# Second self attention: the maxima products of a step are issued after the value products

## The chip, the cores and the metric

One core of a Trainium2 chip runs the whole program. The metric is the device time of one execution in microseconds (us); lower is better. TensorE is called PE in the profile, its weight loads PEld, VectorE DVE, ScalarE ACT, GpSimd POOL and SyncE SP.

## The reference, cut to what matters

The model has four layers on x of shape (2, 1024, 256), each a cross attention and a feed-forward part with experts. The change lies in the first half of layer 1's feed-forward block, a self attention over 1024 tokens with 16 heads of 16 columns in each of 2 batches:

```python
h = _layernorm(x, ln1_g, ln1_b)
qkv = h @ w_qkv + b_qkv                      # (2, 1024, 768)
q, k, v = jnp.split(qkv, 3, axis=-1)         # 16 heads of 16 columns each
scores = jnp.einsum('bqhd,bkhd->bhqk', q, k) / np.sqrt(DK)
attn = jax.nn.softmax(scores, axis=-1)
o = jnp.einsum('bhqk,bkhd->bqhd', attn, v).reshape(B, S, D)
x = x + o @ w_o + b_o
```

## The kernel before, in words

The stages follow one another, and this attention is the stage `quad_attention` (L1499), called "heads1". It takes the 32 pairs of batch and head in 8 groups of four heads. A group has 16 steps (two halves of 512 queries by 8 blocks of 128 keys), so there are 128 steps, t = 0 to 127.

In a step TensorE makes four **scores** (L1627), each 128 keys by 512 queries for one head. ScalarE takes the exponential of each (L1672) into `probs`. There are three score buffers, so the fourth score of a step waits for the exponential of the first. A step later TensorE multiplies the four probabilities with the **values** (L1636, eight instructions in the trace, four column strips side by side) and accumulates over 8 steps into one buffer, `sums_ps`. At the end of 8 steps ScalarE copies that buffer to `sums` (L1664). That copy stands in ScalarE's order behind the second exponential of step t when t is 9, 17, 25 and so on, and the values issued in that same step (the first of the next eight) wait for it (L1634).

The softmax needs the largest score of each query beforehand. It comes from **peaks**, rough scores in bf16 (L1605): a peak is two products of 128 queries by 512 keys, and VectorE reduces it to two maxima per query (L1688). Each group needs 32 peaks. They are made ahead of their group: 40 before the first step, and two in each of the steps 0 to 107. When a group's peaks are reduced, VectorE makes their negated maxima (L1692), and TensorE **turns** them (TURN, L1610), VectorE splits them into two rows (L1699, L1701), and SP puts them by DMA into rows of `q` (L1580). TURN of group g stands at step 16g - 4. When a group's sums are complete TensorE turns them as well (FOLD, eight transposes, L1614) and VectorE divides them by the row sums (L1711, L1715). FOLD of group g stands at step 16(g + 1) + 2, so 18, 34, up to 114, and the last at the end.

Peaks, TURN and FOLD share one pair of buffers, `shared_ps`, and take them in turn. The function `share` (L1593) issues such an item on TensorE. It first waits until VectorE has read the item before the last:

```python
two = shared_ps[:, used % 2, :, :]
if used >= 2:
    pe.wait_ge(shared_read, used - 1)
```

The lists `work_at[t]` (L1526 to L1532) give the items of each step, the peaks first. TensorE's order is written out at L1644 to L1656. In a step with two peaks and a TURN or a FOLD, the peaks are items 0 and 1 and the other one is item 2. VectorE's and ScalarE's own orders, and SP's, are not touched.

Of the kernel before, what the change touches and what calls it, by code (L numbers as in the profile page):

```python
# [1498 lines left out]
def quad_attention(nc, core, name, q_dram, k_dram, values, q_narrow, k_narrow, out):  # L1499
# [17 lines left out]
    def place(g):  # L1517
        b, c, x = g // 4, g // 2 % 2, g % 2
        return b, c, x

    def heads_of(g):
        b, c, x = place(g)
        return [b * H16 + GH * c + 2 * r + x for r in range(QUAD)]
# [15 lines left out]
    with Stage(nc, name) as st:  # L1539
# [23 lines left out]
        @block.sync  # L1563
        def _(sp):
            def load(g):
                u = g % 2
                n = heads_of(g)
                if g >= 2:
                    sp.wait_ge(score_done, QUAD * PER * (g - 1))
                for i, (q_part, k_part) in enumerate(((0, 0), (0, 1), (1, 0), (1, 1))):  # L1570
                    for dst, src, part in ((q, q_dram, q_part), (k, k_dram, k_part)):
                        sp.dma_start(dst[i * HD16:(i + 1) * HD16, u, :, :].bitcast(F32),
                                     src[part, n[0]:n[-1] + 1:2, :, :].rearrange("h w s -> w h s")
                                     ).then_inc(loaded[u], 16)

            def load_max(g):
                u = g % 2
                sp.wait_ge(max_ready, g + 1)
                for r in range(2):
                    sp.dma_start(q[HL + r:HL + r + 1, u, :, :].rearrange("o h s -> o (h s)").bitcast(F32),  # L1580
                                 max_rows[:, r, :].bitcast(F32)).then_inc(max_loaded[u], 16)

            load(0)
            load(1)
            load_max(0)
            for g in range(1, GROUPS):
                if g >= 2:
                    load(g)
                load_max(g)

        @block.tensor
        def _(pe):
            def share(item):  # L1593
                used = number[item]
# [3 lines that stand above are left out]
                if item[0] == PEAK:  # L1598
                    _, g, s, x, pair = item
                    b, c, odd = place(g)  # L1600
                    for i in range(2):
                        r = 2 * pair + i
                        rows = slice(32 * r, 32 * (r + 1))
                        at = b * S + s * P
                        done = pe.matmul(two[:, i, :], q_narrow[rows, c, at:at + P],  # L1605
                                         k_narrow[rows, odd, c, b * S + x * 512:b * S + (x + 1) * 512],
                                         start=True, stop=True, tile_position=(32 * r, 0))
                elif item[0] == TURN:
                    pe.wait_ge(minus_ready, item[1] + 1)
                    done = pe.transpose(two[0:QUAD * BT, 0, 0:P], minus_max[:], core.ident[:])  # L1610
                else:
                    pe.wait_ge(sums_copied, HALVES * (item[1] + 1))
                    for s in range(BT):
                        done = pe.transpose(two[:, s // 4, s % 4 * P:(s % 4 + 1) * P],  # L1614
                                            sums[:, s // 4, s % 4 * P:(s % 4 + 1) * P], core.ident[:])
                done.then_inc(shared_done, 1)

            def score(t, r):
                g, half, c = t // PER, t % PER // BT, t % BT
                u = g % 2  # L1620
                if t % PER == 0 and r == 0:
                    pe.wait_ge(loaded[u], 16 * LOADS * (g // 2 + 1))
                    pe.wait_ge(max_loaded[u], 32 * (g // 2 + 1))
                i = QUAD * t + r
                if i >= RING:
                    pe.wait_ge(exp_done, i - RING + 1)
                pe.matmul(score_ps[:, i % RING, :], k[:, u, r, c * P:(c + 1) * P],  # L1627
                          q[:, u, r, half * 512:(half + 1) * 512], start=True, stop=True).then_inc(score_done, 1)

            def value(t):  # L1630
                g, c = t // PER, t % BT
                pe.wait_ge(exp_done, QUAD * (t + 1))
                if c == 0 and t:
                    pe.wait_ge(sums_copied, t // BT)  # L1634
                for r, n in enumerate(heads_of(g)):
                    done = pe.matmul(sums_ps[r * SIDE:(r + 1) * SIDE, :], values[:, n, c, :],  # L1636
                                     probs[:, t % SLOTS_OF_PROBS, r, :], start=(c == 0), stop=(c == BT - 1),
                                     tile_position=(0, r * SIDE))
                done.then_inc(value_done, 1)

            pe.wait_ge(ones_done, 1)
            for item in work_at[-1]:
                share(item)
            for t in range(STEPS):  # L1644
                items = work_at[t]
                for r in range(QUAD):
                    score(t, r)
                for item in items[0:2]:
                    share(item)
                if t:  # L1650
                    value(t - 1)
                for item in items[2:]:
                    share(item)
            value(STEPS - 1)
            for item in work_at[STEPS]:
                share(item)  # L1656
# [22 lines left out]
        def _(dve):  # L1679
            def take(item):  # L1680
                used = number[item]
                two = shared_ps[:, used % 2, :, :]
                dve.wait_ge(shared_done, used + 1)
                if item[0] == PEAK:
                    _, g, s, x, pair = item
                    if g >= 2 and (s, x, pair) == (0, 0, 0):
                        dve.wait_ge(minus_ready, g - 1)
# [1441 lines left out]
```

## Time and profile before

| | us |
|---|---|
| median of 3 runs | 2937.05 |
| lowest and highest | 2929.41 and 2939.92 |
| the profiled execution | 2941.6 |
| its span from the first to the last instruction | 2939.9 |
| mean granted clock of TensorE in it | 0.864 of full speed |

The profile is of one execution. Its first part gives each engine's busy time, the second cuts the span in 40 slices; further views give the waits, the instructions in order of time and the busy time of chosen stretches. Times of rows are microseconds from the start of the span. The attention of the change takes the span from 1131 (first peak) to 1591; its 128 steps begin at 1181.5.

### The profile page before, as it was taken

The page shows a single profiled execution, that of the slowest core. Times are in us where ns is not written, and L with a number is a line of the kernel's source. Part 1 is how long each engine was busy: PE and PEld are TensorE (multiplying, and loading weights), DVE is VectorE, ACT ScalarE, POOL GpSimd, SP SyncE. Part 2 cuts the span into 40 slices and gives each one's busy share as a digit, 9 for nine tenths or more (in the row PEclk, how much of TensorE's full clock was granted, in tenths as well). Part 3 has the DMA queues.
Part 4 walks back from the last instruction along what each step waited for, and adds up shares of the span by engine and source line. Part 5 has one row for each costly group of instructions (what it writes and reads, how often), then busy time and mean ns, then how long its engine had stood idle before and what let it go on. Part 6 is the DMA issues. An engine that isn't in the chain of part 4 may idle for free. (4 is left out here: it accounts for less than half of the span.)

```text
span 2939.9 us, 36703 instructions
## 1 busy us (share of the span) xinstructions
PE 2249.7 (77%) x12230; PEld 1326.8 (45%) x12231; DVE 1380.5 (47%) x2584; ACT 1085.4 (37%) x2179; POOL 543.6 (18%) x517
## 2 busy tenths in 40 slices
PE   4989999874485965999998289994938999481597
PEld 2423233223383432233334189992327999231354
DVE  4666666616415358578771500003641000458565
ACT  2413333321131630466675144442613444151211
POOL 0204443440141041000000022220002222104011
PEclk8979999987697885599999599997968999685799
DMA  1000000001351035042420466642046664200001
GB/s 59 1 1 9 12 9 12 12 22 58 116 174 33 1 113 72 4 56 31 58 30 6 145 224 198 197 147 76 1 144 209 199 201 156 72 1 30 9 12 36
DMA packets 145705, 216.37 MB, mean 74 GB/s; under 512 B 39840, under 2 KB 101980, under 8 KB 145580
## 3 DMA queue, kind: packets, MB, share of 16 engines
q1 hardware_dynamic: 135884, 188.27, 23.5%
q0 software_dynamic: 9696, 26.49, 2.4%
q8 instruction: 72, 1.18, 0.2%
q14 instruction: 53, 0.43, 0.1%
HBM read 182.00 MB, written 30.15 MB: 72 GB/s over the span
## 5 line engine op out<-in xcount | busy, mean ns | idle before, releaser
L2840 PE MATMUL experts_up_ps<-experts_rowT,experts_w 128*128 128x128 f32 x2864 | 342.4, 278 | 0.0
L1688 DVE TENSOR_REDUCE heads_part_max<-heads_shared_ps 128x2 f32<-128x1024 f32 x256 | 299.9, 1219 | 90.0 <-PE heads_shared_ps L1605 90.0
L1672 ACT ACTIVATE heads_probs<-heads_score_ps 128x512 f32<-128x512 f32 x512 | 266.4, 602 | 190.7 <-PE heads_score_ps L1627 190.7
L2840 PEld LDWEIGHTS experts_up_ps<-experts_rowT,experts_w 128*128 128x128 f32 x2864 | 334.4, 195 | 0.2
L2990 DVE TENSOR_TENSOR experts_y<-experts_down_ps,experts_b_now 128x256 f32<-128x256 f32 x78 | 33.1, 425 | 557.3 <-PE experts_down_ps L2850 557.3
L2900 ACT ACTIVATE experts_hT<-experts_up_ps,experts_b_now 128x128 f32<-128x128 f32 x624 | 223.2, 368 | 48.3 <-PE experts_up_ps L2840 11.4
L1423 DVE TENSOR_REDUCE heads_part_max<-heads_shared_ps 128x1 f32<-128x367 f32 x384 | 181.1, 532 | 125.8 <-PE heads_shared_ps L1313 125.2
L1627 PE MATMUL heads_score_ps<-heads_q,heads_k 66*128 66x512 f32 x512 | 197.5, 473 | 29.7 <-ACT heads_probs L1672 25.5
L1404 ACT ACTIVATE heads_probs<-heads_score_ps 128x1024 f32<-128x1024 f32 x128 | 131.0, 1024 | 217.8 <-PE heads_score_ps L1340 215.3
L2850 PE MATMUL experts_down_ps<-moe_w,experts_hT 128*128 x808 | 184.5, 379 | 0.0
L2789 POOL DMA_INDIRECT y_dram<-experts_y,experts_index x101 | 99.5, 985 | 456.8 <-DVE experts_y L2990 411.3
L1627 PEld LDWEIGHTS heads_score_ps<-heads_q,heads_k 66*128 66x128 f32 x512 | 92.0, 200 | 198.5 <-ACT heads_probs L1672 163.6
L1352 PE MATMUL heads_sums_ps<-heads_probs,self_values 128*64 128x512 f32 (+1 forms) x576 | 159.1, 630 | 0.3 <-ACT heads_probs L1401 0.2
L2850 PEld LDWEIGHTS experts_down_ps<-moe_w,experts_hT 128*128 128x128 f32 x808 | 148.9, 190 | 17.8
L1340 PE MATMUL heads_score_ps<-self_qT,self_kT 64*128 64x512 f32 (+1 forms) x576 | 155.0, 617 | 0.0
L1636 PE MATMUL heads_sums_ps<-heads_probs,self_values 128*32 128x512 f32 x1024 | 146.8, 647 | 4.1 <-ACT heads_sums L1664 4.1
L2850 PE MATMUL experts_down_ps<-l1f_w,experts_hT 128*128 x624 | 141.0, 379 | 0.0
L873 POOL IOTA gate_offset<- 128x128 f32 x3 | 1.1, 356 | 742.4 <-POOLq L55 742.4
L1279 POOL TENSOR_TENSOR core_xT<-core_xT,heads_probs 128x1024 f32<-128x1024 f32 x48 | 122.6, 2554 | 82.5 <-ACT heads_probs L1404 80.5
L2850 PEld LDWEIGHTS experts_down_ps<-l1f_w,experts_hT 128*128 128x128 f32 x624 | 115.7, 190 | 14.1
L2783 POOL DMA_INDIRECT experts_row<-rows_dram,experts_index x101 | 98.8, 978 | 81.6 <-DVE experts_index L2981 46.2
L2881 ACT ACTIVATE experts_rowT<-experts_rowT_ps 128x256 f32<-128x256 f32 x62 | 23.8, 384 | 242.6 <-PE experts_rowT_ps L2830 242.4
(561 smaller groups left out, 3375.4 us busy)
## 6 DMA issues: line engine op xcount, KB each, us to landing
experts_w<-in_L_ffn_W SPq DMA_DIRECT2D x39, 1024.0 KB, 5.3
experts_w<-in_L_ffn_w SPq DMA_DIRECT2D x39, 1024.0 KB, 5.2
experts_w<-in_L_ffn_W SPq DMA_DIRECT2D x23, 512.0 KB, 4.1
core_xT<-y_dram SPq DMA_DIRECT2D x20, 512.0 KB, 4.8
experts_b_now<-in_L_ffn_b SPq DMA_DIRECT2D x78, 128.0 KB, 3.3
heads_q<-l_queries SPq DMA_DIRECT2D x32, 256.0 KB, 10.1
heads_k<-l_keys SPq DMA_DIRECT2D x32, 256.0 KB, 11.9
l1f_w<-in_L_ffn_W SPq DMA_DIRECT2D x8, 1024.0 KB, 11.8
```

Source lines behind the costliest of these rows:

```text
L1279: pool.tensor_tensor(total, first, probs[:, t % SLOTS_OF_PROBS, :, :], ALU.add).then_inc(pool_added, 1)
L1340: done = pe.matmul(score_ps[0:rows, t % 2, r, :], kT[of, c, b, chunk * P:chunk * P + rows], qT[of, c, queries(t)[1]], start=False, stop=Tr ...
L1352: done = pe.matmul(sums_ps[HW * r:HW * (r + 1), :], values[0:rows, b * spec.heads + 2 * c + r, chunk, :], probs[0:rows, t % SLOTS_OF_PROBS ...
L1404: act.activation(probs[:, t % SLOTS_OF_PROBS, :, :], score_ps[:, t % 2, :, :], ACT.Exp, scale=SC).then_inc(exp_done, 1)
L1423: dve.tensor_reduce(part_max[:, g % 2, r, s, x:x + 1], bank[:, 0:PIECE], AX.X, ALU.max).then_inc(shared_read, 1)
L1627: pe.matmul(score_ps[:, i % RING, :], k[:, u, r, c * P:(c + 1) * P], q[:, u, r, half * 512:(half + 1) * 512], start=True, stop=True).then_ ...
L1636: done = pe.matmul(sums_ps[r * SIDE:(r + 1) * SIDE, :], values[:, n, c, :], probs[:, t % SLOTS_OF_PROBS, r, :], start=(c == 0), stop=(c == ...
L1672: act.activation(probs[:, t % SLOTS_OF_PROBS, r, :], score_ps[:, i % RING, :], ACT.Exp, scale=SC).then_inc(exp_done, 1)
L1688: dve.tensor_reduce(part_max[:, g % 2, 2 * pair:2 * pair + 2, s, x], two, AX.X, ALU.max).then_inc(shared_read, 1)
L2840: done = pe.matmul(up_ps[:, f % 4, 0:SLOT], w1_sb[:, u, c, f * P:(f + 1) * P], rowT[:, u % 2, c, :], start=(c == 0), stop=(c == DC - 1))
L2850: done = pe.matmul(down_ps[:, u % 2, 0:D], hT[:, u % 2, f, :], second.sb[:, bass.ds(e, 1), f, :].rearrange("p o d -> p (o d)"), start=(f = ...
L2900: act.activation(hT[:, u % 2, f, :], up_ps[:, f % 4, 0:SLOT], func, bias=bias).then_inc(act_done, 1)
```

## The change

In each step the two items that stood between the scores and the values are issued behind the values, in front of the next step's scores, together with a third item where there is one. Number and form of all instructions stay the same.

```diff
@@ -1645,11 +1645,9 @@
                 items = work_at[t]
                 for r in range(QUAD):
                     score(t, r)
-                for item in items[0:2]:
-                    share(item)
                 if t:
                     value(t - 1)
-                for item in items[2:]:
+                for item in items:
                     share(item)
             value(STEPS - 1)
             for item in work_at[STEPS]:
```

## Rows read from the trace of the kernel before

**Rows 1.** The page: the span, and TensorE's granted clock in 40 slices

```profile
span 2939.9 us, 36703 instructions
...
PEclk8979999987697885599999599997968999685799
```

**Rows 2.** The waits from 1181 to 1590: in total, times, longest

```profile
ACT heads_probs L1672 <- PE heads_score_ps L1627: 190.7, 128, 58.0
...
PEld heads_shared_ps L1610 <- DVE heads_part_max L1688: 8.3, 7, 1.7
PEld heads_shared_ps L1614 <- DVE heads_part_max L1688: 7.4, 6, 1.2
```

**Rows 3.** In order of time: a plain step at full clock (start, length, engine, instruction)

```profile
1317.35 0.96 PE L1627 MATMUL heads_score_ps<-heads_q,heads_k 66*128 66x512 f32 x3
1318.53 0.49 PE L1627 MATMUL heads_score_ps<-heads_q,heads_k 66*128 66x512 f32 x1 [0.22 <-ACT heads_probs L1672]
1318.96 0.40 PE L1605 MATMUL heads_shared_ps<-self_k_narrow,self_q_narrow 32*128 32x512 bf16 x4
1319.28 1.06 PE L1636 MATMUL heads_sums_ps<-heads_probs,self_values 128*32 128x512 f32 x8
...
1319.39 2.36 DVE L1688 TENSOR_REDUCE heads_part_max<-heads_shared_ps 128x2 f32<-128x1024 f32 x2 [0.58 <-PE heads_shared_ps L1605]
1320.28 0.96 PE L1627 MATMUL heads_score_ps<-heads_q,heads_k 66*128 66x512 f32 x3
```

**Rows 4.** In order of time: a late step without peaks, full clock

```profile
1536.44 0.49 PE L1627 MATMUL heads_score_ps<-heads_q,heads_k 66*128 66x512 f32 x1 [0.22 <-ACT heads_probs L1672]
1536.87 0.16 PEld L1636 LDWEIGHTS heads_sums_ps<-heads_probs,self_values 128*32 128x32 f32 x8 [0.24 <-issue]
```

**Rows 5.** In order of time: step 34 with a FOLD, full clock

```profile
1305.99 0.39 PE L1605 MATMUL heads_shared_ps<-self_k_narrow,self_q_narrow 32*128 32x512 bf16 x4
...
1307.70 1.09 PE L1614 MATMUL heads_shared_ps<-core_ident,heads_sums 128*128 128x128 f32 x8 [0.32 <-DVE heads_part_max L1688]
1308.55 0.95 PE L1627 MATMUL heads_score_ps<-heads_q,heads_k 66*128 66x512 f32 x3
```

**Rows 6.** In order of time: values that wait for the copy, with and without peaks

```profile
1253.52 0.39 PE L1605 MATMUL heads_shared_ps<-self_k_narrow,self_q_narrow 32*128 32x512 bf16 x4
...
1254.15 1.06 PE L1636 MATMUL heads_sums_ps<-heads_probs,self_values 128*32 128x512 f32 x8 [0.24 <-ACT heads_sums L1664]
...
1546.87 0.49 PE L1627 MATMUL heads_score_ps<-heads_q,heads_k 66*128 66x512 f32 x1 [0.23 <-ACT heads_probs L1672]
...
1547.94 1.06 PE L1636 MATMUL heads_sums_ps<-heads_probs,self_values 128*32 128x512 f32 x8 [0.57 <-ACT heads_sums L1664]
```

**Rows 7.** In order of time: step 12 with a TURN, half clock

```profile
1237.60 0.61 PE L1605 MATMUL heads_shared_ps<-self_k_narrow,self_q_narrow 32*128 32x512 bf16 x4
...
1238.15 1.94 PE L1636 MATMUL heads_sums_ps<-heads_probs,self_values 128*32 128x512 f32 x8
...
1240.02 0.40 PE L1610 MATMUL heads_shared_ps<-core_ident,heads_minus_max 128*32 128x128 f32 x1
```

**Rows 8.** Stretches: length, busy PE, PEld, DVE, ACT, POOL, then granted clock, DMA

```profile
1181.00:1240.20 59.20, 58.65 (x202) 18.75 (x202) 30.44 (x27) 27.50 (x53) 0.00 (x0) 0.50 0.00 1
1240.40:1533.00 292.60, 265.04 (x1577) 93.92 (x1575) 233.58 (x220) 202.36 (x393) 0.00 (x0) 1.00 0.37 45
...
244.80:247.00 2.20, 0.03 (x1) 0.00 (x1) 2.20 (x3) 0.80 (x1) 1.94 (x2) 1.00 0.00 0
247.00:250.40 3.40, 3.40 (x9) 1.21 (x11) 1.51 (x5) 0.00 (x0) 1.70 (x1) 0.50 0.04 1
...
461.60:463.60 2.00, 0.01 (x1) 0.01 (x1) 2.00 (x3) 0.59 (x1) 1.74 (x2) 1.00 0.04 12
463.60:467.00 3.40, 3.40 (x18) 1.15 (x18) 2.15 (x7) 0.79 (x1) 1.71 (x1) 1.00 0.04 1
...
978.40:980.00 1.60, 0.00 (x1) 0.03 (x1) 1.39 (x3) 1.39 (x2) 0.00 (x0) 1.00 0.01 5
981.00:984.20 3.20, 3.20 (x17) 0.55 (x16) 1.28 (x1) 1.11 (x2) 0.00 (x0) 0.50 0.00 0
```

**Rows 9.** In order of time: transposes after a stall, layer 1's cross attention

```profile
980.00 1.11 PE L546 MATMUL x_banks<-core_ident,x_minus_max 128*128 128x128 f32 x8 [1.60 <-DVE x_heads_out L774]
```

## The prediction, made before the change was run

> **What bounds the kernel now.** I began with the page: the span of 2939.9 us and the row of TensorE's clock [rows 1]. The stage of the change lies in slices 16 to 22 of the 40, and its first slices stand at 5 tenths of the clock. The stretches say where exactly: from 1181 to 1240.2 the granted clock is 0.50 (1.2 GHz), from 1240.4 to 1533 it is 1.00 (2.4 GHz) [rows 8]. The waits come next. ScalarE waits 190.7 us for scores, once in each of the 128 steps (58.0 of it is one wait ahead of the first) [rows 2]. So ScalarE is not the bound; TensorE's own order is.
>
> Then one plain step in order of time [rows 3]. Scores begin at 1317.35, the fourth at 1318.53 (1.18 later, it waits for the first exponential), peaks at 1318.96 (0.43), values at 1319.28 (0.32), the next scores at 1320.28 (1.00). A step is 2.93 us, and its four parts stand one behind the other on TensorE. VectorE reduces the two peaks in 2.36 us and then idles 0.58 us for the next ones. So it has slack too, though not much.
>
> **The change, part by part.** All prices come from the profiled execution, 2941.6 us as a run, 4.6 above the median of 2937.05. I add the sum to the median.
>
> *Plain steps: nothing.* The order scores, peaks, values becomes scores, values, peaks. Nothing in the step waits for the values sooner (their probabilities are a step old), and nobody waits for the maxima within the step. The three changes from one form of product to another stay three. Fourth score to values without peaks takes 0.43 [rows 4], as fourth score to peaks does [rows 3]. Values to something other than scores shows at half clock: values to TURN is 1.87 [rows 7]. Values to peaks at full clock, and peaks to scores, are not shown in the plain step. The nearest rows are 1.00 (values to scores) and 0.32 (peaks to values) [rows 3], and I take those, so the step stays at 2.93. I allow 0.05 us a step either way, which over the 95 full-clock steps with peaks (13 to 107) is 5 us down or up. VectorE sees the same spacing, so its two waits on `shared_read` stay met.
>
> *Steps with a FOLD: +1.00 each.* The third item must wait until VectorE has reduced the first peak of the same step. Now the values lie between them. In step 34 peaks start at 1305.99, FOLD at 1307.70, so 1.71 later, and TensorE still idles 0.32 after the values [rows 5]. Behind the change the peaks come after the values and FOLD directly behind the peaks. The 1.71 remains, because it is TensorE's peaks plus one reduction, but the values' 1.00 us no longer lies inside it. It now stands ahead. There are six such FOLDs (steps 18 to 98), the six waits of the row for L1614 [rows 2]: 6 x 1.00 = 6.0 us.
>
> *Steps with a TURN: +1.00 each at full clock, +1.35 at half clock.* It is the same wait: seven in the row [rows 2], of which those in steps 12, 28, up to 92 stand behind peaks; the seventh, in step 108, does not. Five run at full clock: 5.0 us. Step 12 is at half clock: peaks to values 0.55, values to TURN 1.87, no wait [rows 7]. After the change TURN can come some 1.9 us behind the peaks (0.65 until the reduction starts, by estimate 0.22 more than at full clock, then half of the 2.36), in place of 0.55 from the peaks to the values: 1.35. TURN's DMA on SP, which brings the maxima into `q`, comes about 1 us later but has four steps to spare. What queues behind the waiting item on TensorE is the next step's scores, and ScalarE behind those.
>
> *Steps with the copy (9, 17, up to 105): +0.32 each.* The values wait for ScalarE's copy. Now the peaks pass ahead of them and fill part of that wait: peaks at 1253.52, values at 1254.15, which is 0.63 and not 0.32. Without peaks the values come 1.07 behind the fourth score and not 0.43 [rows 6]. So the whole wait of 0.64 will be bare where 0.31 was. Thirteen steps at 0.32 make 4.2 us. Steps 113 and 121 have no peaks and stay.
>
> *Other ends.* In step 1 the peaks wait less for VectorE (some -0.3). TURN at 108 and FOLD at 114 only swap with the values: 0.
>
> The sum is 6.0 + 5.0 + 1.35 + 4.2 - 0.3 = 16.3 us, so 2953.4 us, 0.55% more. A measurement of this kernel can tell about 0.5% (14.7 us, so 2922.4 and 2951.7) from no change.
>
> *The clock.* A FOLD step will contain a bare stall. The peaks end some 0.33 behind their start and FOLD comes at 1.71, so 1.38 us without products, then 0.85 us of transposes [rows 5]. In the first attention TensorE did nothing from 244.8 to 247.0 and the clock was 0.50 in the 3.4 us after; another stall, 461.6 to 463.6, was followed by a clock of 1.00 [rows 8]. In layer 1's cross attention 1.60 us of idle time followed by transposes ended in a clock of 0.50 as well [rows 8, 9]. So 1.38 idle and 0.85 of transposes lie near the edge, between a case that fell and one that did not, if transposes keep the clock up as little as idle time does.
>
> The Trainium skill says just that of transposes, in "TensorE: Matmul & The Clock Gate", Part 4: a transpose through TensorE "doesn't count as PE-busy the same way". By that rule FOLD's stall is 2.2 us to the clock, and some FOLDs drop it; if it did not hold, only 1.38 us would count and the sum would stay 2953. The row at 980.00 [rows 9] agrees with it, since the clock fell after 1.60 us of idle plus transposes.
>
> What a fall costs is bounded in two places. In the first attention it lasted 3.4 us, so at most 1.7 us lost. In this attention the loop stayed at half clock from 1181.5 to 1240.0, through steps 0 to 12 [rows 7, 8]: 58.5 us, where 13 plain steps at full clock would be 38.1. That is 20.4 us, 1.57 a step. I take two falls among the six FOLDs, of three steps each, 2 x 3 x 1.57 = 9.4 us: between the two ends, since either row may be the nearer one. The forecast is 16.3 + 9.4, some 25 us over the median, 2962 us. The ends of this term are 0 and about 60 (three falls of 20.4).
>
> **The rivals.**
>
> *Waits only, 2953 us.* The clock does not care for FOLD's 1.38 us of idle. For it: the stall at 461.6 that was followed by full clock. Against it: the falls after 2.2 us and after 1.60 us with transposes [rows 8, 9]. With the 5 us of the unseen changes of form it spans 2948 to 2958. Chance 0.28.
>
> *Long half clock, 2975 to 3013 us.* A fall lasts like the first thirteen steps, 20 us each, one to three of them. For it: in those steps the loop stayed at 0.50 with TensorE busy for 58.65 of 59.20 us [rows 8]. Against: the fall at 247, which was over after 3.4 us, and that the FOLDs are only 16 steps apart, so that three such falls would cover nearly the whole loop. Chance 0.20.
>
> *The clock rises earlier, 2933 to 2942 us, not slower than before.* The steps at half clock at the start are worth up to 20.4 us. If the new neighbours (values and peaks together, then the dense first scores) let the clock rise in the first steps, that pays for the 16.3. It decides from a rise 10 steps (16.3 / 1.57) earlier than now. For it: nothing in the rows says what made the clock rise at 1240.3, and the runs of before spread over 10.5 us. Against: the products per step are the same. Chance 0.10.
>
> **How the numbers follow.** The forecast case (waits, and some short falls, 2955 to 2975) has 0.42. The predicted time is its 2962. The range is 2944 to 2995: below it lies most of the early rise, above it the longer half of the long half clock. Slower by over 0.5%: nearly all of the forecast case, a little over half of waits only, all of long half clock, together 0.70. Faster by over 0.5% needs an early rise and cheaper changes of form as well: 0.03. The rest, 0.27, is within 0.5%.
>
> **What would show it.** Right: a plain step of 2.93 us, with values 0.43 behind the fourth score and peaks 1.00 behind the values; FOLD and TURN 1.71 behind their peaks with some 1.3 us of TensorE idle time each in place of 0.32; L1636 waiting about 0.57 for the copy in thirteen more steps; and stretches at 0.50 that begin behind FOLDs. Wrong: a plain step of another length, a FOLD that starts sooner than 1.6 us behind the peaks, or a clock of 1.00 from the first steps on.

## The result and the profile after

The changed kernel took 3018.39 us (median of 5 runs, 3011.92 to 3041.07), the kernel before 2937.05. The ratio is 1.029, 95% interval 1.0251 to 1.033: slower by 2.9%, outside the stated range of 2944 to 2995. The profiled execution was the longest of the five, 3041.07 us. In the ratios of this document, which compare means, runs more than 1.5% above the fastest of their kernel are left out, but not in the medians; this concerns one run each of the second and the sixth experiment and two of the four of the fifth, for which no ratio is given.

Every wait came out as worked out. What was far too small was the term for the clock. Here are lines of the page of the changed kernel, with its span and the clock in 40 slices (before: [rows 1]):

```profile
span 3039.3 us, 36703 instructions
...
PEclk8979999985887876955876769997987999786699
```

The slices of this attention, 16 to 22 counted from one, read 5, 5 and then nines before; now they read 6, 9, 5, 5, 8, 7, 6. The busy time and clock of chosen stretches of the loop say where the time is (columns as in [rows 8]):

```profile
1181.00:1199.40 18.40, 17.65 (x59) 6.35 (x59) 8.03 (x7) 8.54 (x17) 0.00 (x0) 0.50 0.00 1
1199.40:1281.40 82.00, 70.75 (x421) 24.52 (x419) 62.72 (x60) 54.73 (x107) 0.00 (x0) 1.00 0.22 27
1281.40:1472.60 191.20, 183.24 (x645) 60.31 (x641) 95.19 (x89) 81.92 (x159) 0.00 (x0) 0.50 0.28 34
1472.60:1554.40 81.80, 70.55 (x421) 24.52 (x419) 62.58 (x60) 54.52 (x107) 0.00 (x0) 1.00 0.22 27
1554.40:1653.50 99.10, 96.95 (x330) 32.04 (x327) 37.18 (x35) 45.31 (x88) 0.00 (x0) 0.50 0.18 22
1653.50:1687.00 33.50, 30.06 (x153) 10.80 (x151) 1.05 (x2) 25.95 (x51) 0.00 (x0) 1.00 0.00 1
```

TensorE spent 309 us of the loop at 0.50 (18.4 + 191.2 + 99.1), where before it was 59 [rows 8]. Those 249.5 us more, at a loss of 1 - 2.93/4.62 (a plain step at full and at half clock), are 91 us. With the 16.3 of the sum that is 107 to 108. The first to the last score took 404.0 us before (1181.6 to 1585.6) and 505.2 now (1181.8 to 1687.0), 101 more, and the span grew by 99.4. The 6 us between fit the steps with waits, which the half clock stretches less: a copy step takes 3.58 us at full and 4.96 at half clock (1.39 times), a plain step 2.93 and 4.62 (1.58 times).

In order of time, the values that wait for the copy, a FOLD step and a plain step of the changed kernel, all at full clock (answering to [rows 6, 5, 3]):

```profile
1240.05 0.50 PE L1627 MATMUL heads_score_ps<-heads_q,heads_k 66*128 66x512 f32 x1 [0.22 <-ACT heads_probs L1670]
1241.12 1.06 PE L1636 MATMUL heads_sums_ps<-heads_probs,self_values 128*32 128x512 f32 x8 [0.57 <-ACT heads_sums L1662]
...
1243.62 0.50 PE L1627 MATMUL heads_score_ps<-heads_q,heads_k 66*128 66x512 f32 x1 [0.22 <-ACT heads_probs L1670]
1244.05 1.07 PE L1636 MATMUL heads_sums_ps<-heads_probs,self_values 128*32 128x512 f32 x8
1245.05 0.39 PE L1605 MATMUL heads_shared_ps<-self_k_narrow,self_q_narrow 32*128 32x512 bf16 x4
1246.76 1.09 PE L1614 MATMUL heads_shared_ps<-core_ident,heads_sums 128*128 128x128 f32 x8 [1.32 <-DVE heads_part_max L1686]
1247.61 0.95 PE L1627 MATMUL heads_score_ps<-heads_q,heads_k 66*128 66x512 f32 x3
1248.78 0.51 PE L1627 MATMUL heads_score_ps<-heads_q,heads_k 66*128 66x512 f32 x1 [0.22 <-ACT heads_probs L1670]
...
1250.21 0.39 PE L1605 MATMUL heads_shared_ps<-self_k_narrow,self_q_narrow 32*128 32x512 bf16 x4
1250.54 0.96 PE L1627 MATMUL heads_score_ps<-heads_q,heads_k 66*128 66x512 f32 x3
1251.72 0.49 PE L1627 MATMUL heads_score_ps<-heads_q,heads_k 66*128 66x512 f32 x1 [0.23 <-ACT heads_probs L1670]
```

From fourth score to fourth score the plain step takes 2.94 us (1248.78 to 1251.72). FOLD starts 1.71 behind its peaks, with 1.32 us idle in place of 0.32. The first fall of the clock comes like this, in order of time:

```profile
1276.28 1.07 PE L1636 MATMUL heads_sums_ps<-heads_probs,self_values 128*32 128x512 f32 x8
1277.28 0.39 PE L1605 MATMUL heads_shared_ps<-self_k_narrow,self_q_narrow 32*128 32x512 bf16 x4
1278.99 0.28 PE L1610 MATMUL heads_shared_ps<-core_ident,heads_minus_max 128*32 128x128 f32 x1 [1.32 <-DVE heads_part_max L1686]
1279.03 0.93 PE L1627 MATMUL heads_score_ps<-heads_q,heads_k 66*128 66x512 f32 x3
...
1281.79 0.61 PE L1605 MATMUL heads_shared_ps<-self_k_narrow,self_q_narrow 32*128 32x512 bf16 x4
1282.33 2.28 PE L1627 MATMUL heads_score_ps<-heads_q,heads_k 66*128 66x512 f32 x4
```

A bare stall of 1.32 us ahead of TURN, step 28. From 1281.4 on everything is slow: the peaks take 0.61 in place of 0.39. The clock stayed there for 191 us, although TensorE was busy for 183 of them. The second fall, at 1554.4, follows the TURN of step 92.

### The profile page after: what moved, and what is told of

Its sections match the earlier page's. It is cut to its first block and busy times, and to the rows that moved or that the text cites. A ratio compares the mean times of both kernels' runs of the same rounds, so it can differ in the third digit from the quotient of the medians.

```text
span 3039.3 us, 36703 instructions
## 1 busy us (share of the span) xinstructions
PE 2348.3 (77%) x12230; PEld 1356.6 (45%) x12231; DVE 1380.9 (45%) x2584; ACT 1070.7 (35%) x2179; POOL 543.8 (18%) x517
## 3 DMA queue, kind: packets, MB, share of 16 engines
q8 instruction: 72, 1.18, 0.2%
## 5 line engine op out<-in xcount | busy, mean ns | idle before, releaser
L1627 PE MATMUL heads_score_ps<-heads_q,heads_k 66*128 66x512 f32 x512 | 239.1, 579 | 18.2 <-ACT heads_probs L1670 14.0
L2898 ACT ACTIVATE experts_hT<-experts_up_ps,experts_b_now 128x128 f32<-128x128 f32 x624 | 208.1, 367 | 81.8 <-PE experts_up_ps L2838 65.3
L1636 PE MATMUL heads_sums_ps<-heads_probs,self_values 128*32 128x512 f32 x1024 | 190.6, 827 | 6.2 <-ACT heads_sums L1662 6.2
L1627 PEld LDWEIGHTS heads_score_ps<-heads_q,heads_k 66*128 66x128 f32 x512 | 115.1, 250 | 142.0 <-ACT heads_probs L1670 87.9
```

Of the source, the lines that this page charges most:

```text
L2898: act.activation(hT[:, u % 2, f, :], up_ps[:, f % 4, 0:SLOT], func, bias=bias).then_inc(act_done, 1)
```

## The experiments

The theory: the peaks behind the values leave a bare stall (TensorE idle, with nothing issued in it) ahead of each TURN and FOLD; such a stall often lowers the clock; and this loop does not soon raise it again. The main rival: the new order of the plain steps is what keeps the clock low. Each experiment but the last two, which are single runs, has its own median and one of the kernel before on the same chip. "Dense products" are bf16 products of 128 rows by 128 columns by 512 whose results are overwritten.

**1 and 2. Each half of the change alone.** In the first the plain steps have the new order and the item steps the old one, in the second the other way round: there the condition is `len(items) < 3`. The diff is that of the first.

```diff
+                first = items[0:2] if len(items) != 2 else []
+                for item in first:
+                    share(item)
                 if t:
                     value(t - 1)
-                for item in items:
+                for item in items[len(first):]:
```

> The new order in the plain steps, the old one in the twelve steps that have a TURN or a FOLD behind peaks. Theory (the clock falls because TensorE stands bare for 1.32 us between peaks and a TURN or FOLD): no such stall, no fall. What is left of the change is the copy's wait in thirteen steps, 4.2 us, so 2935 to 2945 us, and a clock of 1.00 from its first rise to the end of the loop. Rival (the new order of plain steps is itself what keeps the loop at half clock): it stays near the changed kernel, 3000 us or more, with long stretches at 0.50.

> The other half: the new order only in the twelve steps that have a TURN or a FOLD behind peaks, the old one in all others. Theory (bare stall, then fall): 12 us for the waits and falls behind one or more TURNs, so 2975 us or more, with stretches at 0.50 that begin within 3 us behind a TURN or FOLD. Rival (plain order decides): 2950 us, the twelve waits of 1.0 us alone, and no fall.

The first took 2973.56 us against 2941.09 (1.0107, 1.0075 to 1.0139), the second 2990.76 (1.0138, 1.0083 to 1.0194, with runs from 2964 to 3019). The second came out as the theory had it: its clock fell at 1447.1, as the TURN of step 76 started, for 10 us, and at 1501.7, at the end of the stall ahead of the TURN of step 92, for 102 us. Its plain steps have the old order, so a long stretch at half clock does not need the new one. The first did not come out: 2973.56 is 29 us over the upper end of what was expected. Its trace, in order of time, shows why:

```profile
1538.84 0.50 PE L1627 MATMUL heads_score_ps<-heads_q,heads_k 66*128 66x512 f32 x1 [0.22 <-ACT heads_probs L1673]
1540.15 0.22 DVE L1693 TENSOR_REDUCE heads_minus_max<-heads_part_max 128x32 f32<-128x64 f32 x1
...
1540.52 0.27 PE L1610 MATMUL heads_shared_ps<-core_ident,heads_minus_max 128*32 128x128 f32 x1 [1.18 <-DVE heads_minus_max L1693]
```

Step 108 has a TURN and no peaks, and this kernel left it in the old order behind a step in the new one. The last peaks were reduced late, TURN waited for the maxima with nothing ahead of it, TensorE stood bare for 1.18 us, and at 1542.2 the clock fell for the rest of the loop. So the experiment had a stall of its own making. An earlier fall, at 1252.0 for 3.4 us, came 0.35 us behind the start of a peak that TensorE had waited 0.51 us for.

**3. The same lateness, but not bare.**

```diff
                 for item in items:
+                    if len(items) == 3 and item is items[2]:
+                        for _ in range(5):
+                            score(t + 1, 0, False)
                     share(item)
```

> The changed kernel, and between the peaks and the TURN or FOLD of the twelve steps TensorE issues the next step's first score five times over (its result is the same, the last one counts). TURN and FOLD come as late as before, 1.7 us behind the peaks, but TensorE is busy for about 1.1 of the 1.32 us. Theory (idle time lowers the clock): no fall, so the waits alone remain, 2940 to 2958 us. Rival (the lateness itself, or the order of plain steps, costs the time): near 3018 us.

2947.9 us (2943.76 to 2969.01) against 2941.09: 1.0037, 0.9993 to 1.0081. The profiled run took 2950.94. As chosen stretches:

```profile
1187.00:1205.00 18.00, 17.80 (x59) 6.34 (x59) 8.21 (x7) 8.72 (x17) 0.00 (x0) 0.50 0.00 1
1205.00:1592.00 387.00, 351.05 (x2015) 128.88 (x2015) 258.62 (x245) 260.94 (x507) 0.00 (x0) 1.00 0.28 34
```

No fall in this run; the run of 2969.01 was not profiled, so it may have had one. TURN and FOLD come as late as in the changed kernel, only the idle time is gone, and with it some 70 of the 81 us. This run also prices the waits: the scores take 405.6 us (1187.2 to 1592.8) against 404.0 before, with 41 us less at half clock, worth 15.0 us. So the waits cost 1.6 + 15.0 = 16.6 us, where 16.3 were forecast.

**4. TURN and FOLD ahead of the values and peaks.** The items of a step are sorted so that its TURN or FOLD comes first, and the step is scores, TURN or FOLD, values, peaks.

```diff
+    for t in range(STEPS):
+        work_at[t].sort(key=lambda item: item[0] == PEAK)
...
+                first = [item for item in items if item[0] != PEAK]
+                for item in first:
+                    share(item)
                 if t:
                     value(t - 1)
-                for item in items:
+                for item in items[len(first):]:
```

> TURN or FOLD ahead of the peaks of its step: scores, TURN or FOLD, values, peaks; plain steps in the new order. Neither waits for a peak of its own step. Theory: no bare stall, no fall, and the 12 us of waits gone too; against the kernel before it loses 4.2 us at the copies and gains 12 times 0.38 us of idle time, so 2925 to 2945 us. Rival (plain order): 3000 us or more.

2999.85 us (2996.13 to 3005.51) against 2941.09, 1.0201. By its number this looks like the rival's win. In order of time:

```profile
1230.83 0.50 PE L1629 MATMUL heads_score_ps<-heads_q,heads_k 66*128 66x512 f32 x1 [0.22 <-ACT heads_probs L1675]
...
1232.51 0.37 PE L1612 MATMUL heads_shared_ps<-core_ident,heads_minus_max 128*32 128x128 f32 x1 [1.18 <-DVE heads_minus_max L1695]
```

It has the same fault as the first. TURN no longer waits for a peak of its own step, but for the maxima that include the last peaks of the step before, with only four scores between. The stall of 1.18 us is bare again, and each of the four falls (47.8, 30.7, 3.4 and at least 79 us long) begins within 0.4 us of the start of one of the seven TURNs. The FOLDs, which wait for nothing there (four of them at full clock), are followed by none. So it speaks against the rival after all, though it wasn't built for that.

**5 and 6. Only the TURNs filled, only the FOLDs filled.** The condition of the third experiment with one more term; the sixth has FOLD in place of TURN.

```diff
-                    if len(items) == 3 and item is items[2]:
+                    if len(items) == 3 and item is items[2] and item[0] == TURN:
```

> The changed kernel with the five extra first scores only ahead of the six TURNs; the six FOLDs keep their bare stall of 1.32 us. All falls seen so far in the changed kernel came behind TURNs. Theory (only a TURN's stall lowers the clock): as with both filled, 2943 to 2955 us, no fall. Rival (a FOLD's stall with its 0.85 us of transposes does it too, as predicted): stretches at 0.50 that begin behind FOLDs, 2970 us or more.

> The counterpart: the extra scores only ahead of the six FOLDs, the TURNs keep their bare stall. Theory (only TURNs): falls behind TURNs and long stretches at 0.50, 2990 to 3030 us. Rival (FOLDs cause part of them): clearly below 3018 us, 2960 to 2985.

Fifth: 2994.76 us with runs of 2981, 3008, 2949 and 3041; sixth: 2986.0 with runs from 2966 to 3016, both against 2937.76. The sixth lies just between the two ranges of its expectation and decides nothing by its time. "Only a TURN's stall" fell with the fifth. Its profile in order of time, and the stretch behind it:

```profile
1298.91 0.39 PE L1605 MATMUL heads_shared_ps<-self_k_narrow,self_q_narrow 32*128 32x512 bf16 x4
1300.62 1.97 PE L1614 MATMUL heads_shared_ps<-core_ident,heads_sums 128*128 128x128 f32 x8 [1.32 <-DVE heads_part_max L1691]
1302.24 2.25 PE L1627 MATMUL heads_score_ps<-heads_q,heads_k 66*128 66x512 f32 x4
```

```profile
1300.40:1375.60 75.20, 74.43 (x257) 25.58 (x257) 37.16 (x36) 32.42 (x63) 0.00 (x0) 0.50 0.26 31
```

The clock fell at the end of the FOLD's bare stall, ahead of its transposes. In the sixth it fell four times, each behind the start of a TURN, for 6.8, 17.1, 30.7 and 10.2 us. Both kinds of stall do it, then, and how long a fall lasts is scattered so widely that the four runs of the fifth lie up to 92 us apart.

**7. Dense products ahead of the first step, in the kernel before.**

```diff
             for item in work_at[-1]:
                 share(item)
+            for n in range(20):
+                pe.matmul(score_ps[:, n % RING, :], q_narrow[:, 0, 0:P], k_narrow[:, 0, 0, 0:512], start=True, stop=True)
```

> The kernel before, with twenty dense products (bf16, 128 rows by 128 columns by 512) put behind the last item ahead of step 0, where TensorE otherwise waits 4.2 us for a DMA; they write into score buffers that are overwritten. Nothing else changes. Theory (this loop does not raise the clock by itself but holds it once it is at 1.00, and dense products raise it): step 0 or 1 runs at 1.00, the 20 us of the first thirteen steps are saved less 1 to 3 us by which the products outlast the wait, so 2915 to 2928 us. Rival (the loop's rise at 1240 had another cause, or the clock falls again in the first steps): 2937 to 2945 us.

2927.82 us against 2937.76, 9.9 us less by the medians and 5.4 by the means: 0.9982, 0.9962 to 1.0001. In its profile the clock rose at 1180.9 within the products, fell again at 1187.7 behind a wait of 0.51 us in step 1, and was back at 1198.0 to stay. So the direction is the theory's and the median just inside its range (2915 to 2928), but the interval reaches 1: by itself this run does not show a gain.

**8. The first experiment without its own stall.** `len(items) == 3` in place of `!= 2`.

> As the first experiment, but step 108 (a TURN without peaks) has the new order too, values ahead of the TURN, so that the one bare wait of 1.18 us there is gone. Theory: the fall at 1542 us of the first experiment, which lasted 92 us, is gone, and the plain steps' new order alone costs the copy's 4.2 us and some 3 us at the seams between the orders: 2938 to 2952 us. Rival (new plain order lowers the clock by itself): stays at 2973 us.

2950.36 us (2942.10 to 2962.17) against 2937.76: 1.0049, 1.0023 to 1.0074, within the 2938 to 2952 expected. Against the first experiment that one step was worth about 20 us. What is left is 12.6 us: 4.2 at the copies, and at the seams, where a step in the old order follows one in the new, the second peak waits 0.52 us for VectorE, eleven times, 5.7 us in all (that view of the waits is below).

```profile
PE heads_shared_ps L1605 <- DVE heads_part_max L1689: 5.7, 11, 0.5
```

The clock was not left alone, though. In the profiled run it fell at 1446.3 for 3.4 us and at 1480.5 for 30.7 us, 0.2 and 1.0 us behind the start of such a second peak; the second fall in order of time:

```profile
1479.44 0.39 PE L1605 MATMUL heads_shared_ps<-self_k_narrow,self_q_narrow 32*128 32x512 bf16 x2 [0.52 <-DVE heads_part_max L1689]
1479.76 1.30 PE L1636 MATMUL heads_sums_ps<-heads_probs,self_values 128*32 128x512 f32 x8
1480.98 0.40 PE L1610 MATMUL heads_shared_ps<-core_ident,heads_minus_max 128*32 128x128 f32 x1
```

The values are already slow, before TURN is issued. So a wait of 0.52 us was enough here. As the main cause the rival fails all the same: with the new order in 96 plain steps the time is 68 us below that of the changed kernel, of which the waits explain only some 7 (12.4 at TURN and FOLD less 5.7 at the seams), and both falls came behind waits that the seams made.

**9. Stalls left bare, and dense products in the next step.**

```diff
                     score(t, r)
+                if t and len(work_at[t - 1]) == 3:
+                    pe.wait_ge(exp_done, QUAD * (t + 1) - RING + 1)
+                    for _ in range(8):
+                        pe.matmul(score_ps[:, QUAD * (t + 1) % RING, :], q_narrow[:, 0, 0:P],
+                                  k_narrow[:, 0, 0, 0:512], start=True, stop=True)
                 if t:
```

> The changed kernel with eight dense products (bf16, 128 rows by 128 columns by 512, into a score buffer that is overwritten) ahead of the values of each step that follows a TURN or FOLD step. The stalls stay bare, so the clock may fall; the products cost 12 times 1.7 us and a wait of some 0.6 us for an exponential each, about 28 us, at full clock. Theory (what makes a fall dear is that this loop does not raise the clock again by itself for tens of us, and dense products do): stretches at 0.50 behind an item end within about 8 us, and the total is 2953 + 28, so 2975 to 2995 us. Rival (the long stretches have another cause): long stretches stay and the 28 us come on top, over 3035 us.

2978.4 us (2973.85 to 2983.01) against 2939.46: 40 us less than the changed kernel, although the dense products add some 23 us even at full clock (12 steps of 1.89, as values come 2.32 us and not 0.43 behind the fourth score, 1283.26 to 1285.58). The stretches at half clock behind the start, as chosen:

```profile
1248.40:1251.60 3.20, 3.15 (x7) 1.22 (x8) 0.25 (x1) 1.48 (x4) 0.00 (x0) 0.51 1.08 122
...
1395.20:1398.60 3.40, 3.40 (x9) 1.02 (x8) 0.00 (x0) 0.92 (x2) 0.00 (x0) 0.50 0.04 10
...
1419.20:1422.60 3.40, 3.40 (x9) 1.04 (x8) 0.00 (x0) 0.99 (x3) 0.00 (x0) 0.51 1.04 116
...
1531.80:1535.20 3.40, 3.38 (x8) 1.37 (x9) 0.22 (x1) 1.45 (x3) 0.00 (x0) 0.50 1.05 117
```

The clock fell four times, as often as in the worst of the others, each time 1.7 to 2.4 us behind the start of a TURN (once) or a FOLD (three times), and each time it was back after about 3.4 us. Of the 21 falls of the other traces, only four were over as soon. This bears out the second half of the theory. A fall itself is cheap; dear is that this loop, though TensorE is busy for nearly all of it, can leave the clock at 1.2 GHz for long.

**10. The start again, with step 1 mended:** three more such products into `sums_ps` ahead of the peaks of step 1.

> The kernel before with the twenty dense products ahead of step 0, as in the seventh experiment, and three more ahead of the peaks of step 1, where TensorE stood idle for 0.51 us and the clock fell again at 1187.8 and came back at 1198. Theory: no second fall, 10 us at half clock less, which is 3 to 4 us less time: 2920 to 2926 us against 2938 before. Rival (the clock falls in the first steps all the same): 2927 to 2938 us.

2927.92 us (12 runs, 2921.49 to 2941.15) against 2939.46 of the kernel before (17 runs): 0.9965, interval 0.9944 to 0.9986. It is 0.35% faster than the kernel before, the lowest ratio of the study and the only one whose whole interval lies below 1. The median lies above the 2920 to 2926 expected and in the rival's range of 2927 to 2938, though the profiled run (2925.21 us) shows what the theory said. As chosen stretches:

```profile
1177.50:1182.60 5.10, 5.10 (x14) 1.83 (x13) 1.35 (x3) 0.00 (x0) 0.00 (x0) 0.51 0.02 6
1182.60:1568.00 385.40, 349.09 (x2026) 124.02 (x2024) 266.73 (x251) 269.73 (x524) 0.00 (x0) 1.00 0.28 34
```

The whole loop runs at 1.00. The median is not below that of the seventh (on another chip), so no run shows that the three products more are worth anything. The gain of 11.5 us is below the 18 one would work out from the first profile; the start at half clock differs between runs (next), which may be part of it.

**11 and 12. Both kernels once more, for their profiles.**

> The changed kernel once more, for its profile. Theory: falls begin within 3 us behind a bare stall at a TURN or a FOLD again, but not at the same ones, and the time differs with the length of the stretches at half clock. Rival (the falls are fixed in the program): the same stretches as in the first profile, from step 28 and from step 92.

> The kernel before once more, for its profile. Theory: half clock at the start of the steps, ending at another step than 12, since nothing in step 12 is dense; no fall until the end of the loop. Rival: it ends in step 12 again, so that TURN has to do with it.

The changed kernel took 3005.45 us, the kernel before 2949.13, one run each. The changed one's stretches at half clock:

```profile
1232.20:1235.60 3.40, 3.40 (x15) 0.94 (x7) 1.18 (x2) 1.22 (x3) 0.00 (x0) 0.51 0.05 12
...
1283.40:1348.20 64.80, 62.79 (x219) 21.09 (x220) 31.87 (x31) 28.10 (x55) 0.00 (x0) 0.50 0.28 33
...
1409.60:1474.40 64.80, 62.92 (x220) 21.08 (x220) 31.88 (x30) 28.24 (x55) 0.00 (x0) 0.50 0.28 34
```

The falls belong to the TURNs of steps 12, 28 and 60: the first begins 1.8 us behind the start of TURN, the other two within 0.3 us of it. In the first profile they followed 28 and 92, and that of step 12 went by unharmed. The same program falls at other stalls in another execution. The two profiled runs of the changed kernel, 3005 and 3041 us, stand on either side of its median. Its loop took 452.8 us in this one (1183.6 to 1636.4). The kernel before had half clock until 1227 in place of 1240, and no fall afterwards; its loop took 399.6 us, 53 less than the changed one's, while the spans differ by 56. Outside the loop the fourteen traces differ by up to 17 us, so whole times of single runs tell little of the loop.

## Why the prediction was wrong

**The waits were right.** FOLD and TURN 1.71 us behind their peaks, 1.32 us idle, the plain step 2.94 us, the values 1.07 behind the fourth score where they wait for the copy (1240.05 to 1241.12). From fourth score to fourth score at full clock, a FOLD step grew from 4.17 to 5.17 us, a TURN step from 3.37 to 4.37 (at half clock from 4.67 to 6.05) and a copy step from 3.25 to 3.58. For the sum of 16.3 us the third experiment measures 16.6. The changes of form that no row showed (values to peaks 1.00, peaks to scores 0.33) cost what their nearest rows said.

**The step that failed is the term for the clock:** "two falls among the six FOLDs, of three steps each, 2 x 3 x 1.57 = 9.4 us". The mechanism was right, a bare stall and then half clock. Its size was wrong, and its place too. The profiled run had two falls, but of 191.2 and 99.1 us, which is some 60 steps and not 6, and both stood behind TURNs. They cost about 106 us at the loss worked out above, where 9.4 stood in the sum. The rival "long half clock" had the right cause at 0.20 and was priced from the first thirteen steps at 20 us a fall, which is short of these two as well (70 and 36 us). Against it the prediction said that three such falls "would cover nearly the whole loop". That was a slip, for three times thirteen steps are 39 of 128; and with the start the stretches at half clock did cover 309 of 505 us. The rows that should have decided were there: [rows 8] showed this loop busy for 58.65 of 59.20 us at 0.50, and nothing that ended it. A stretch whose end nothing explains is one sample of a length and bounds it on neither side. The 20 falls of all traces that had no dense products near them lasted from 3.4 to 191 us, twelve of them over 30. Short ones as at 247.0, then, do happen in this loop, but they are the minority.

**Which stalls lower the clock.** In the five traces with bare stalls of 1.32 us and no dense products behind them (the changed kernel twice, and experiments 2, 5 and 6 for what each left bare) a TURN met at full clock came with a fall 11 times of 21, a FOLD once of 17. The prediction had named FOLDs alone, by the Trainium skill's rule that a transpose "doesn't count as PE-busy the same way" ("TensorE: Matmul & The Clock Gate", Part 4). These counts do not bear it out: after the same 1.32 us of idle time, 0.85 us of transposes was rather the milder case. How much milder is open, for experiment 9, where the falls began before or just as the dense products did, had one fall in six TURNs and three in six FOLDs; with it the counts are 12 of 27 and 4 of 23. Why is not settled either.

**How long the stalls were.** In all fourteen traces together the clock fell 25 times between the first and the last score, always between 0.4 us before and 2.5 us behind the start of an instruction that TensorE had stood idle for. Of stalls met at full clock, those of 1.32 us came with a fall 16 times of 50, those of 1.18 us (TURN in experiments 1 and 4) 5 of 8, those of 0.51 to 0.52 us ahead of a second peak (experiments 1, 7 and 8) 4 of 24. The 47 of 0.32 us ahead of a TURN or FOLD and the 120 of 0.57 to 0.58 us ahead of values that wait for the copy had none. So the length alone does not decide; what else does was not tested.

**The third rival was partly right, unseen.** With the new order of plain steps the first rise came at 1199.5 and 1204.8 in the two profiles of the changed kernel, and at 1240.3 and 1227.0 in the two of the kernel before. Of the seven other profiles with the new plain order, experiments 3, 5, 8 and 9 rose by 1205.0, experiment 4 at 1215.0, and 1 and 6 at 1224.7 and 1229.9; experiment 2, with the old one, at 1245.7. On average that is 29 us earlier, worth some 11 us, and helps to explain why the third experiment ends only 7 us over the kernel before. It is a tendency over twelve executions; no experiment was made for its cause.

## What to carry to other kernels

Before moving work behind a wait, ask what TensorE does while it waits. Against the kernel before, the same lateness cost 7 us filled and 81 bare, because a bare stall of 1.2 to 1.3 us, and at times one of 0.5, can take the clock to 1.2 GHz, and a loop like this one may then stay there for tens of microseconds while it looks fully busy. Look at the granted clock of a loop's stretches first; if it starts at half, a few dense products of no use, put where TensorE waits anyway, can be a cheap speed-up (here 11 of 2939 us).

## What the runs showed of the hardware that was not expected

- Stalls of 1.32 us came with a fall to half clock in one execution and not in another of the same program (the TURN of step 12 in the two profiles of the changed kernel), and so did 4 of 24 stalls of 0.52 us; full clock came back after 3.4 us where eight dense products followed, and after 3.4 to 191 us where they did not.
- A busy TensorE is no sign of full clock: 183.24 of 191.20 us busy at 0.50.
- Twenty products of 128 rows by 128 columns by 512 in bf16 were issued when the clock rose in both traces that had them, 5.1 and 4.8 us after the first (1177.5 to 1182.6 in experiment 10, 1176.1 to 1180.9 in experiment 7).
